# A graph network step kernel on one core: filter products as a pair, and an order of stores and waits

## Chip, cores and metric

One Trainium2 chip (trn2), one core of it. The metric is the device time of one execution in microseconds. The engines go by the profile's names: PE is TensorE (PEld its weight loads), DVE is VectorE, ACT is ScalarE, POOL is GpSimd, SP is SyncE, whose queue here issues nearly all plain transfers.

## The reference

Two graph layers over 50000 nodes and 50000 edges, 128 channels, all in float32. `src` is random, `dst` is sorted.

```
h = relu(layernorm(x));  basis = exp(-coef * (edge_weight - centers)^2)      # 50 centres
ef = (softplus(basis @ Wf1 + bf1) - log 2) @ Wf2 + bf2                       # the filter, per edge
agg = segment_sum((h @ W_lin.T)[src] * ef, dst)                              # messages
x1 = x + (softplus(agg @ Wm1 + bm1) - log 2) @ Wm2 + bm2
h = relu(layernorm(x1))
out = x1 + h @ W_self.T + b_self + segment_mean over src of (h @ W_neigh.T + b_neigh)[dst]
```

## The kernel before

The 50000 rows are padded to 50176 and cut into 98 quads of 512 rows (4 tiles of 128). A first stage counts and sorts indices. The second, which the change touches, is a software pipeline of 98 + 18 steps: in step s every engine does one piece of work for each of several quads, of quad s, s - 1 and so on to s - 18. A last stage sums the edge rows by their `src` bins. `over_steps` (line 98) writes the first 20 steps out, then loops of four steps, and again peeled steps at 72 to 75 and at the end; each engine has a `step` function in which the order of its work is written by hand, and semaphores are the only ties between engines. An engine's instructions, and a queue's, run in the order written; a wait holds all that is behind it.

For quad q as edges: POOL gathers rows of `x` by `src` into `xg` (step q, `gather`); DVE makes their statistics (`row_stats`, `row_aggr`); in step q + 1 DVE and ACT make the inverse root, and the filter: TensorE's `filter_up` (line 1105) multiplied the basis by `Wf1` into `u_ps` in step q, ACT makes `clamp`, `exponential` and `logarithm` (`lu`) of it, DVE's `soften` makes `su`, and TensorE's product with `wf2` goes to `filt_ps`, on top of a bias row (`bias_row(filt_ps, 0, 0)`). ACT makes `xn`, TensorE turns it (`turn`, into `turn_ps`), ACT copies it out as `hT` and the filter as `efs` (named `efb` in rows). In step q + 2 TensorE projects `hT` with `wlin` into `proj_ps`; in step q + 3 DVE's `message` multiplies the two into `msgw` and SP stores it (`store_msg`, line 708). A basis tile holds two quads, on partitions 0 to 49 and 64 to 113 (`BASIS_AT`), and ACT makes it in every even step (`make_basis`).

For quad j as nodes, steps j + 7 to j + 13: SP loads four windows of the message table (`load_windows`, line 718, `win`), DVE looks at their `dst` column (`window_dst`, line 873, `rel`), makes one-hots (`one_hots`, `hot`), TensorE sums (`block_sums`, half-height products, line 1118), ACT copies to `aggs`, TensorE makes the nu product (line 1152), `nsu` follows as for the filter, the product with `wm2`, DVE's `residual` (`x1`, `x` in rows), its layer norm (`node_norm`, `comb` in rows), a transpose, `nhT`, and two products with it: with `wneigh` into `neigh_ps`, from which DVE's `hidden_out` (line 906) makes `h1s` that SP stores (`store_h1`, line 703, table `h_table`), and with `wself` into `self_ps`, from which `node_out` makes `y` rows. `y` rows are stored by `store_y` until quad 61 and kept in SBUF from there (step 72 on). `self_ps`, `mlp_ps` and `neigh_ps` are one bank (`node_ps`), so the bias row of `self_ps` may be written only when `hidden_out` has read the neighbour product; its wait is `wait_used(pe, n_hn, s - 10, 1)`, line 1170, ahead of the bias rows of both `filt_ps` and `self_ps`, which are a pair on rows 0 to 2 and 64 to 66.

For quad q as edges again, steps q + 15 to q + 18: SP loads `dst` keys and four windows of h1 rows (`load_keys`, `load_hidden`, `hwin`), DVE makes one-hots (`edge_hots`, `hotT`), TensorE picks rows (`edge_rows`, half-height, line 1130), ACT makes `row_out`, POOL scatters it (line 798).

Eight PSUM banks: 0 `u_ps`, 1 `turn_ps`, 2 `proj_ps`, 3 `filt_ps`, 4 and 5 the window sums and edge rows by halves, 6 `nu_ps`, 7 `node_ps`.

TensorE's order in a step: product with `wself` (s - 11), block sums (s - 8), product with `wm2` (s - 9), edge rows (s - 17), nu (s - 8), `filter_up` (s), product with `wneigh` (s - 11), transpose of `comb` (s - 10), product with `wlin` (s - 2), the two bias rows, product with `wf2` (s - 1), transpose of `xn` (s - 1). SP's: x rows, y store, edge weights in even steps, message windows, keys, hidden windows, message store, h1 store. DVE's begins with `hot`, `hotT`, `h1s`, message and ends with statistics.

## Time and profile before

| | us |
|---|---|
| median of 3 runs | 1825.5 |
| lowest and highest | 1819.09, 1832.73 |
| the profiled execution | 1825.08 |
| its span, first to last instruction | 1822.9 |
| PE busy | 1614.5 (89%) |
| DVE busy | 1478.6 (81%) |
| ACT busy | 1086.3 (60%) |
| POOL busy | 1114.7 (61%) |
| SP: queue of transfers q1 | 255.35 MB, 48.6% of the 16 DMA engines' time |

A busy share is an average over stages with other limits; instructions that only wait or issue a transfer are not counted as busy, so SP has no busy time, and its load has to be read from its own waits and its timeline. A row of the timeline gives the start, the time to the end of the last instruction merged into it, and in brackets the idle time of the engine before it and who ended it. TensorE's weight loads and matmuls overlap; a float32 product has two records for each matmul, and their ends are modelled, so distances between starts are used for what a product takes.

### The profile page before, as it was taken

The page shows a single profiled execution, that of the slowest core. Times are in us where ns is not written, and L with a number is a line of the kernel's source. Part 1 is how long each engine was busy: PE and PEld are TensorE (multiplying, and loading weights), DVE is VectorE, ACT ScalarE, POOL GpSimd, SP SyncE. Part 2 cuts the span into 40 slices and gives each one's busy share as a digit, 9 for nine tenths or more (in the row PEclk, how much of TensorE's full clock was granted, in tenths as well). Part 3 has the DMA queues.
Part 4 walks back from the last instruction along what each step waited for, and adds up shares of the span by engine and source line. Part 5 has one row for each costly group of instructions (what it writes and reads, how often), then busy time and mean ns, then how long its engine had stood idle before and what let it go on. Part 6 is the DMA issues. An engine that isn't in the chain of part 4 may idle for free. (4 is left out here: it accounts for less than half of the span.)

```text
span 1822.9 us, 49666 instructions
## 1 busy us (share of the span) xinstructions
PE 1614.5 (89%) x13156; PEld 1256.6 (69%) x13156; DVE 1478.6 (81%) x4720; ACT 1086.3 (60%) x2615; POOL 1114.7 (61%) x938
## 2 busy tenths in 40 slices
PE   2549769999999999999999999999999648888997
PEld 1223246777777777777777777777787548888997
DVE  8998646888888888888888889888887427777886
ACT  1007677877777777777777777777764103333333
POOL 5990144356666666666666776677743536555676
PEclk9769878999999999999999999999999859999999
DMA  3000035577777777777777776766766539999876
GB/s 83 0 0 1 18 79 147 169 215 210 219 220 224 221 221 214 219 222 222 215 216 215 222 207 201 207 198 200 201 188 176 158 113 267 271 270 273 232 219 174
DMA packets 293579, 333.96 MB, mean 183 GB/s; under 512 B 42220, under 2 KB 233710, under 8 KB 293486
## 3 DMA queue, kind: packets, MB, share of 16 engines
q1 hardware_dynamic: 216654, 255.35, 48.6%
q0 software_dynamic: 25088, 51.83, 10.1%
q10 hardware_dynamic: 51744, 25.70, 4.7%
q8 instruction: 39, 0.64, 0.1%
q14 instruction: 54, 0.44, 0.1%
HBM read 212.96 MB, written 119.75 MB: 183 GB/s over the span
## 5 line engine op out<-in xcount | busy, mean ns | idle before, releaser
L787 POOL DMA_INDIRECT xg<-in_x,srcs x392 | 414.6, 1058 | 372.8 <-issue 317.7
L798 POOL DMA_INDIRECT row_table<-row_out,posq x392 | 385.2, 983 | 168.4 <-issue 113.9
L1273 PE MATMUL psum<-bin_rows,bin_hot 128*128 128x129 f32 x2352 | 293.7, 284 | 49.7 <-DVE bin_hot L1246 49.5
L1273 PEld LDWEIGHTS psum<-bin_rows,bin_hot 128*128 128x128 f32 x2352 | 278.3, 197 | 65.2 <-DVE bin_hot L1246 33.7
L1246 DVE TENSOR_TENSOR bin_hot<-iota,bin_rel 128x1536 f32<-128x1536 f32 x98 | 178.6, 1822 | 5.5 <-DVE bin_rel L1243 0.2
L1130 PE MATMUL psum<-hwin,hotT 64*128 64x128 f32 x2352 | 165.5, 289 | 15.7 <-DMA hwin<-h_table 13.6
L1130 PEld LDWEIGHTS psum<-hwin,hotT 64*128 64x128 f32 x2352 | 147.3, 196 | 29.0 <-issue 12.3
L1030 ACT ACTIVATE xn<-xg,shift,rstd 128x128 f32<-128x128 f32 x392 | 161.0, 493 | 2.4 <-DVE shift L852 2.2
L1118 PE MATMUL psum<-hot,win 64*128 64x128 f32 x2352 | 159.7, 283 | 0.7 <-DVE hot L882 0.7
L1118 PEld LDWEIGHTS psum<-hot,win 64*128 64x128 f32 x2352 | 140.8, 190 | 12.9 <-DVE hot L882 1.0
L1096 PEld LDWEIGHTS psum<-wneigh,nhT 128*128 128x128 f32 x784 | 95.8, 191 | 70.2 <-issue 70.0
L1288 ACT ACTIVATE x<-psum,inverse 128x128 f32<-128x128 f32 x200 | 57.2, 368 | 135.3 <-DVE inverse L1256 135.3
L1109 PE MATMUL psum<-basis,wf 50*128 50x512 f32 x196 | 114.3, 664 | 26.4 <-DVE su L859 20.4
L1036 ACT ACTIVATE nhT<-psum 128x512 f32<-128x512 f32 x98 | 58.5, 597 | 124.8 <-PE psum L1102 115.1
L569 ACT ACTIVATE psum<-psum,cols 128x196 f32<-128x196 f32 x130 | 51.1, 393 | 128.0 <-PE psum L544 128.0
L1096 PE MATMUL psum<-wf,su 128*128 128x128 f32 x784 | 117.9, 295 | 0.0
L1096 PEld LDWEIGHTS psum<-wf,su 128*128 128x128 f32 x784 | 98.8, 198 | 23.3 <-issue 23.3
L1007 ACT ACTIVATE nclamp<-psum,cols 128x512 f32<-128x512 f32 x98 | 67.3, 687 | 79.0 <-PE psum L1152 78.1
L1096 PE MATMUL psum<-wm,nsu 128*128 128x128 f32 x784 | 113.5, 288 | 0.0
L1096 PE MATMUL psum<-wneigh,nhT 128*128 128x128 f32 x784 | 113.0, 287 | 0.0
L1288 ACT ACTIVATE nx<-psum,inverse 128x128 f32<-128x128 f32 x192 | 54.9, 369 | 97.0 <-DVE inverse L1256 97.0
L1152 PE MATMUL psum<-aggs,wm 128*128 128x512 f32 x196 | 109.6, 641 | 2.5 <-ACT aggs L1036 2.5
(174 smaller groups left out, 3702.6 us busy)
## 6 DMA issues: line engine op xcount, KB each, us to landing
bin_rows<-row_table SPq DMA_DIRECT2D x196, 195.0 KB, 3.2
win<-msg_table SPq DMA_DIRECT2D x392, 96.8 KB
hwin<-h_table SPq DMA_DIRECT2D x392, 96.0 KB
msg_table<-msgw SPq DMA_DIRECT2D x98, 258.0 KB
nx<-in_x_nodes SPq DMA_DIRECT2D x98, 256.0 KB
h_table<-h1s SPq DMA_DIRECT2D x98, 256.0 KB
y_table<-ys SPq DMA_DIRECT2D x61, 256.0 KB
out<-xg ACTq DMA_DIRECT2D x50, 256.0 KB, 3.8
```

The source lines that it names most:

```text
L787: nc.gpsimd.indirect_dma_start(out=xg[:, par, t, :], out_offset=None, in_=ins["x"], in_offset=bass.IndirectOffsetOnAxis(ap=srcs[:, par, t: ...
L798: nc.gpsimd.indirect_dma_start(out=row_dram, out_offset=bass.IndirectOffsetOnAxis(ap=posq[:, par, t:t + 1], axis=0), in_=row_out[:, par, t ...
L1007: nc.scalar.activation(c, ups, ACT.Relu, bias=high, scale=-1.0).then_inc(done, 1)
L1030: last = nc.scalar.activation(out[:, t, :], source[:, t, :], ACT.Relu, bias=shift_[:, t:t + 1], scale=rstd_[:, t:t + 1])
L1096: last = nc.tensor.matmul(ps[:, t * P:(t + 1) * P], left[:, t * P:(t + 1) * P], weights_[:], start=(b is None), stop=(b is None or t == QT ...
L1109: nc.tensor.matmul(u_ps[:], wf1[at:at + BASIS, :], basis[at:at + BASIS, slot, :], start=True, stop=True).then_inc(e_u, 1)
L1118: last = nc.tensor.matmul(tile_ps(agg_at, 2 * g + h), win[half_of(h), par, g, w, 0:C], hot[half_of(h), par, g, w, :], start=(w == 0), stop ...
L1130: last = nc.tensor.matmul(tile_ps(rows_at, 2 * g + h), hotT[half_of(h), par, g, w, :], hwin[half_of(h), par, g, w, :], start=(w == 0), sto ...
L1152: nc.tensor.matmul(nu_ps[:], wm1[:], aggs[:], start=True, stop=True).then_inc(n_u, 1)
L1246: nc.vector.tensor_tensor(bin_hot[:, par, :, :, :], iota4[:].rearrange("p (b n) -> p b n", b=2).unsqueeze(2).broadcast_to([P, 2, BTILES, B ...
L1273: last = nc.tensor.matmul(bank[2 * slot + b][:, h * MW:(h + 1) * MW], bin_hot[:, slot % 2, b, w, h * P:(h + 1) * P], bin_rows[:, slot, b, ...
L1288: last = nc.scalar.activation(of_slot(means, slot)[:, t, :], sums_of(slot)[:, t // 2, t % 2, 0:C], ACT.Identity, scale=inverse[:, slot, t ...
```

## The change

Banks: `u` gets a second bank (3) for odd quads, and the projection and the filter product share bank 2. `filter_up` runs in even steps only and issues the products of both quads of the basis tile. TensorE's projection moves from behind the transpose of `comb` to behind the edge rows, with a wait for the evacuated filter, and the filter's bias row also waits for the message of the quad before. SP: `store_h1` moves from the end of a step to behind `load_x`, `store_msg` to ahead of `load_hidden`. DVE: `message` and `hidden_out` come ahead of `edge_hots`, and `window_dst` moves to the end of the step.

```diff
--- before.py
+++ after.py
@@ -663,7 +663,9 @@
                 x_keys, x_win, scattered = sa2("x_keys"), sa2("x_win"), sa2("scattered")
                 x_hot, x_sum, x_src, x_pos, x_rows = sa("x_hot"), sa("x_sum"), sa("x_src"), sa("x_pos"), sa("x_rows")
                 x_ones = sa("x_ones")
-                u_ps, turn_ps, proj_ps, filt_ps, _, _, nu_ps, node_ps = bank
+                u_even, turn_ps, edge_ps, u_odd, _, _, nu_ps, node_ps = bank
+                u_of = (u_even, u_odd)
+                proj_ps = filt_ps = edge_ps
                 self_ps = mlp_ps = neigh_ps = node_ps
                 agg_at, rows_at = 0, 2 * P
 
@@ -757,6 +759,8 @@
                     def step(s, even, odd, pair, slot, late):
                         if there(s - 9):
                             load_x(s - 9, odd)
+                        if there(s - 13):
+                            store_h1(s - 13, odd)
                         if there(s - 12) and not kept(s - 12, late):
                             store_y(s - 12, even)
                         if even == 0 and there(s):
@@ -765,12 +769,10 @@
                             load_windows(s - 7, odd)
                         if there(s - 15):
                             load_keys(s - 15, odd)
+                        if there(s - 3):
+                            store_msg(s - 3, odd)
                         if there(s - 16):
                             load_hidden(s - 16, even)
-                        if there(s - 3):
-                            store_msg(s - 3, odd)
-                        if there(s - 13):
-                            store_h1(s - 13, odd)
                     over_steps(sp, step)
                     for p in range(2):
                         sp.wait_ge(h1_stored[p], 16 * (QUADS // 2))
@@ -927,12 +929,12 @@
                     def step(s, even, odd, pair, slot, late):
                         if there(s - 8):
                             one_hots(s - 8, even)
+                        if there(s - 3):
+                            message(s - 3, odd)
+                        if there(s - 12):
+                            hidden_out(s - 12, even)
                         if there(s - 17):
                             edge_hots(s - 17, odd)
-                        if there(s - 12):
-                            hidden_out(s - 12, even)
-                        if there(s - 3):
-                            message(s - 3, odd)
                         if there(s - 10):
                             square_root(s - 10, nroot, nsquare, n_root, n_square)
                         if there(s - 1):
@@ -957,13 +959,11 @@
                             inverse_root(s - 1, factor[:], root[:], rstd[:], e_factor, e_norm, e_rstd)
                         if there(s - 10):
                             inverse_root(s - 10, nfactor, nroot, nrstd, n_factor, None, n_rstd)
-                        if there(s - 7):
-                            window_dst(s - 7, odd)
                         if there(s - 10):
                             node_norm(s - 10, even)
                         if there(s - 1):
                             mean_shift(s - 1, emv[:, odd, :, :], rstd[:], shift[:], e_rstd, e_shift)
-                            soften(s - 1, u_ps[:], bf1_low, ln_out[:], su[:], e_softln, e_filter, e_soft)
+                            soften(s - 1, u_of[odd][:], bf1_low, ln_out[:], su[:], e_softln, e_filter, e_soft)
                         if there(s - 9):
                             residual(s - 9, odd)
                         if there(s):
@@ -981,6 +981,8 @@
 
                             wait_used(dve, n_ln, s - 9, 1)
                             row_aggr(s - 9, nstats, nmv, n_stats, n_aggr)
+                        if there(s - 7):
+                            window_dst(s - 7, odd)
                     nc.vector.memset(row_out[:], 1.0).then_inc(x_ones, 1)
                     dve.wait_ge(x_ones, 1)
                     take_src(0, 0)
@@ -1072,7 +1074,7 @@
                         if there(s - 9):
                             logarithm(s - 9, neu[:], nlu[:], n_exp, n_soft, n_softln)
                         if there(s - 1):
-                            clamp(s - 1, u_ps[:], bf1_top, clampu[:], e_u, e_clamp)
+                            clamp(s - 1, u_of[odd][:], bf1_top, clampu[:], e_u, e_clamp)
                             exponential(s - 1, clampu[:], eu[:], e_clamp, e_exp)
                         if even == 0 and there(s):
                             make_basis(pair, slot)
@@ -1102,11 +1104,12 @@
                             last = nc.tensor.transpose(turn_ps[:, t * P:(t + 1) * P], source[:, t, :], ident[:])
                         last.then_inc(done, 1)
 
-                    def filter_up(q, par, pair, slot):
+                    def filter_up(q, pair, slot):
+
                         pe.wait_ge(basis_ready, pair + 1)
                         wait_used(pe, e_soft, q, 1)
-                        at = BASIS_AT[par]
-                        nc.tensor.matmul(u_ps[:], wf1[at:at + BASIS, :], basis[at:at + BASIS, slot, :], start=True, stop=True).then_inc(e_u, 1)
+                        for par, at in enumerate(BASIS_AT):
+                            nc.tensor.matmul(u_of[par][:], wf1[at:at + BASIS, :], basis[at:at + BASIS, slot, :], start=True, stop=True).then_inc(e_u, 1)
 
                     def block_sums(j, par):
                         pe.wait_ge(n_hot, j + 1)
@@ -1146,12 +1149,15 @@
                             if there(s - 8):
                                 pe.wait_ge(n_aggT, s - 8 + 1)
                             edge_rows(s - 17, odd)
+                        if there(s - 2):
+                            pe.wait_ge(e_filter_sb, s - 2 + 1)
+                            product(s - 2, proj_ps, hT, wlin, None, e_hT, e_msg, e_proj)
                         if there(s - 8):
                             pe.wait_ge(n_aggT, s - 8 + 1)
                             wait_used(pe, n_soft, s - 8, 1)
                             nc.tensor.matmul(nu_ps[:], wm1[:], aggs[:], start=True, stop=True).then_inc(n_u, 1)
-                        if there(s):
-                            filter_up(s, even, pair, slot)
+                        if even == 0 and there(s):
+                            filter_up(s, pair, slot)
                         if there(s - 11):
                             pe.wait_ge(n_y, s - 11 + 1)
                             if there(s - 9):
@@ -1164,14 +1170,13 @@
                                 pe.wait_ge(e_hT, s - 2 + 1)
                             wait_used(pe, n_hT, s - 10, 1)
                             turn(nxn, n_turned)
-                        if there(s - 2):
-                            product(s - 2, proj_ps, hT, wlin, None, e_hT, e_msg, e_proj)
                         if there(s - 10):
                             wait_used(pe, n_hn, s - 10, 1)
                             if at_first(s - 10, 1):
                                 pe.wait_ge(n_x1, s - 9 + 1)
                         if there(s - 1):
                             wait_used(pe, e_filter_sb, s - 1, 1)
+                            wait_used(pe, e_msg, s - 1, 1)
                             bias_row(filt_ps, 0, 0)
                         if there(s - 10):
                             bias_row(self_ps, 2, HALF)
```

## Rows read from the trace of the kernel before

**Rows 1.** The head of the page, and its row of the scatters

```profile
span 1822.9 us, 49666 instructions
...
L798 POOL DMA_INDIRECT row_table<-row_out,posq x392 | 385.2, 983 | 168.4 <-issue 113.9
```

**Rows 2.** The windows: us; busy time of each engine; PEclk; DMA share; GB/s

```profile
381.00:1045.00 664.00, 653.78 (x5684) 508.39 (x5682) 579.09 (x2327) 508.13 (x1105) 451.01 (x441) 1.00 0.75 219
1045.00:1349.00 304.00, 303.68 (x2670) 237.71 (x2669) 270.13 (x1081) 236.50 (x516) 210.63 (x204) 1.00 0.70 200
```

**Rows 3.** Waits of SP's queue, 381:1045: us in total, times, longest

```profile
SPq L81 <- DVE hotT L917: 0.6, 1, 0.6
```

**Rows 4.** Waits of SP's queue, 1045:1349

```profile
SPq L81 <- DVE hotT L917: 12.5, 13, 2.4
```

**Rows 5.** Line 1152 in 381:1043 and in 1042:1349: ns min/median/max, first to last start

```profile
L1152 PE MATMUL psum<-aggs,wm x112: 592/645/697, 381.3 to 1042.5; 128*128 128x512 f32 x112
...
L1152 PE MATMUL psum<-aggs,wm x54: 592/645/697, 1041.9 to 1348.7; 128*128 128x512 f32 x54
```

**Rows 6.** Timeline of PE, part of one step: start us, us, engine, line, out<-in

```profile
1016.89 1.61 PE L1130 MATMUL psum<-hwin,hotT 64*128 64x128 f32 x24
1018.43 1.12 PE L1152 MATMUL psum<-aggs,wm 128*128 128x512 f32 x2
1019.48 1.12 PE L1109 MATMUL psum<-basis,wf 50*128 50x512 f32 x2
1020.54 1.16 PE L1096 MATMUL psum<-wneigh,nhT 128*128 128x128 f32 x8
1021.53 0.60 PE L1102 MATMUL psum<-ident,comb 128*128 128x128 f32 x4
1021.97 1.06 PE L1096 MATMUL psum<-wlin,hT 128*128 128x128 f32 x8
1022.96 0.39 PE L1086 MATMUL psum<-bias,ones 3*128 3x512 bf16 x2
```

**Rows 7.** Timeline of DVE in the same step

```profile
1015.01 0.22 DVE L876 TENSOR_SCALAR rel<-win,qhalf 128x6 f32<-128x6 f32 x1
...
1019.76 0.93 DVE L882 TENSOR_TENSOR hot<-iota,rel 128x768 f32<-128x768 f32 x1
...
1021.73 0.69 DVE L910 TENSOR_TENSOR h1s<-psum,bneigh 128x512 f32<-128x512 f32 x1 [0.17 <-PE psum L1096]
```

**Rows 8.** Waits, 381:1045: us in total, times, longest

```profile
DVE rel L876 <- DMA win<-msg_table: 20.0, 22, 1.9
...
DVE h1s L910 <- DMA h_table<-h1s: 8.9, 16, 1.5
```

**Rows 9.** Timeline after the last filter product: two steps, transpose to bias row

```profile
1369.68 0.60 PE L1102 MATMUL psum<-ident,comb 128*128 128x128 f32 x4
...
1370.96 0.38 PE L1086 MATMUL psum<-bias,ones 3*128 3x512 bf16 x1 [0.68 <-DVE h1s L910]
...
1417.57 0.60 PE L1102 MATMUL psum<-ident,comb 128*128 128x128 f32 x4
1417.77 0.69 DVE L910 TENSOR_TENSOR h1s<-psum,bneigh 128x512 f32<-128x512 f32 x1 [0.47 <-PE psum L1096]
...
1418.52 0.38 PE L1086 MATMUL psum<-bias,ones 3*128 3x512 bf16 x1 [0.35 <-DVE h1s L910]
```

**Rows 10.** Timeline of SP's queue in the last steps

```profile
1440.95 2.47 SPq L754 DMA_DIRECT2D hwin<-h_table  x4
1443.53 0.52 SPq L706 DMA_DIRECT2D h_table<-h1s  x1
...
1447.46 2.91 SPq L754 DMA_DIRECT2D hwin<-h_table  x4
```

**Rows 11.** Timeline while the steps fill

```profile
262.91 0.39 PE L1086 MATMUL psum<-bias,ones 3*128 3x512 bf16 x1
...
265.00 0.66 DVE L870 TENSOR_TENSOR msgw<-psum,efb 128x512 f32<-128x512 f32 x1
```

## The prediction

> **What bounds the kernel now.** I read the table of windows first, then the waits engine by engine, then SP's own queue, and last the timeline of single steps. The profiled span is 1822.9 us [rows 1], and the change touches only the big stage of 116 steps.
>
> TensorE looks like the bound: in 381 to 1045 us it is busy 653.78 of 664 us, in 1045 to 1349 us 303.68 of 304 [rows 2]. But the nu product (line 1152, two records a step) gives the length of a step. Its 112 records are 56 steps, so 55 distances from 381.3 us to 1042.0 us (a step's first record starts 0.5 us before its second, the last one listed): 12.01 us a step. The 54 records of the second stretch are 26 distances from 1041.9 to 1348.2 us: 11.78 us a step [rows 5]. The work on TensorE is the same in both, so in the first stretch something else adds 0.23 us a step, some 12 us.
>
> SP's queue is what differs. In the first stretch it waits 0.6 us in 664 [rows 3]: it issues without a pause, and is the limit. In the second, where `y` rows stay in SBUF and their store is gone, it waits 12.5 us in 304 [rows 4], so its own work is (304 - 12.5) / 25.8 = 11.3 us a step, and TensorE leads with 11.78. SP's lateness comes through where VectorE waits for its transfers: 22 times for window rows (20.0 us), 16 times for the store of the h1 buffer (8.9 us) [rows 8]. I call the stretches SP-led and TensorE-led.
>
> **The change part by part.**
>
> *The pair.* The filter product takes 1020.54 - 1019.48 = 1.06 us a step [rows 6]. After the change an even step issues two on the row halves 0 to 49 and 64 to 113, into two banks, and an odd step none. Two such halves run beside each other here: the 24 half-height records of the edge sums take 1018.43 - 1016.89 = 1.54 us, while 8 full-height ones take 1021.53 - 1020.54 = 0.99 us, so 24 in a row would take 2.97; and a pair of bias rows is busy 0.39 us where a single one is 0.38 [rows 6, 9]. I take 1.06 us for the pair, and so 0.53 us less a step. The bounds are 0 gained (the halves queue) and 0.53.
>
> The Trainium skill bears on this (TensorE: Matmul & The Clock Gate, Part 3: matmuls on distinct row groups run concurrently), and the trace agrees. Against single-row-group products stands another page, TensorEngine Tiling, Key Properties: changing the tiling mode drains the engine. By that rule the change would save two drains more in an odd step; but the filter product follows the full-height one before it and precedes the one behind it at 1.05 and 1.06 us, and no drain is seen, so nothing is added.
>
> *The projection moves ahead of nu.* Its 0.99 us (1022.96 - 1021.97) [rows 6] is neither added nor removed, but it was the cover of a wait. The bias rows overwrite the bank of the neighbour product, so they wait for VectorE to have made `h1s` from it. Between the two stood the transpose and the projection: 1.43 us. After the change only the transpose, 1021.97 - 1021.53 = 0.44 us. What the wait needs is seen in the last steps, where there is no projection either: transpose at 1417.57, `h1s` at 1417.77 as soon as the product is there, bias at 1418.52 [rows 9]. That is 0.95 us with VectorE waiting ready, so 0.95 - 0.44 = 0.51 us of new idle time of TensorE in every step. Queued behind it are the filter product, the transpose of `xn` and the whole next step. This is the crux: 0.53 us saved, 0.51 paid. Bounds of the price: 0, if something I don't see covers it, and 0.9, if VectorE is late by another 0.4 us.
>
> Is VectorE late? In this order it does the window look, `hot`, the message and then `h1s`. It is free at 19.76, where `hot` starts now; with 0.22 for the look, 0.93 for `hot` and 0.69 for the message (as long as `h1s`) [rows 7], it could start `h1s` at 21.6 at the latest. The neighbour product ends in an even step 0.99 us later than now (`h1s` at 22.72) and in an odd one 1.06 earlier than that (21.66), so TensorE's result comes last in both, by 0.1 us in the odd ones. An even step is thus 11.78 + 0.51 = 12.29, an odd one 12.29 - 1.06 = 11.23, the mean 11.76.
>
> *The new wait of the filter's bias row on the message.* The projection now shares the filter's bank. The message comes before `h1s` on VectorE and both are waited for at the same place, so this costs nothing beyond the 0.51. Its cover is gone only while the steps fill: there the bias row ran at 262.91 and the message of that step at 265.00, held up by gathered rows [rows 11]. Against it stands the odd filter product being ready a step early. I take 0, bounds 4 us gained and 5 lost.
>
> *SP's order.* No issue is added or taken away, so SP's 12.01 us a step in the SP-led stretch stay. What changes is how far the engines can run ahead of it. The h1 store goes out some 10 us earlier in a step, which ends the 8.9 us of waits for it [rows 8]; it depends on `h1s` of the step before, which is long done. The message store moves ahead of the four hidden loads, and the message is done by then. Moved past: the hidden loads start one issue later, with a step of slack. The next to be late is the window load, and the look at it moves from 1015.01 to just before `hot` at 1019.76 [rows 7]: 4.75 us more slack. TensorE at 11.76 gains 0.25 us a step on SP's 12.01, 13.8 us in 55 steps, so it uses up the 4.75 us once, after 19 steps, and then keeps SP's pace. In the TensorE-led stretch SP (11.3) catches up. So the SP-led stretch gives 4.7 us; bounds 0 (other waits appear at once) and 12 (it is freed altogether).
>
> *The TensorE-led stretch.* 26 steps at -0.02: 0.5 us.
>
> *The last steps.* From 1349 to 1416 us there is no filter work; transpose to bias takes 1370.96 - 1369.68 = 1.28 us, since `hotT` stands before `h1s` on VectorE [rows 9]. After the change `h1s` comes first: 0.95, so 0.33 us in each of 7 steps, 2.3 us. Behind that, steps are a chain on SP: hidden load at 1440.95, h1 store at 1443.53, and the next hidden load waits for it to land until 1447.46, 6.51 us [rows 10]. With the store ahead of the hidden load that landing is hidden, and the scatters are the limit, 4 * (0.98 + 0.30) = 5.1 us [rows 1]. 1.4 us in three steps, I take 3.5 with what surrounds them; bounds 0 and 6.
>
> *Sum.* 4.7 + 0.5 + 2.3 + 3.5 = 11.0 us less. The profiled execution took 1825.08 us against the median of 1825.5, so 1825.08 - 11.0 = 1814.1: 1814.
>
> **The rivals.**
>
> *The stalls go altogether* (15 in 100). SP's pace was set by its neighbours rather than by itself, and the engines hold 11.76 everywhere: 0.25 * 55 = 13.8 in place of 4.7, so 1805. For it: steps of 11.75 occur between longer ones in that stretch. Against: SP's 0.6 us of waits [rows 3].
>
> *The h1s wait is covered* (12 in 100). TensorE then runs at 11.25 a step, but SP needs 11.3: in 26 steps 0.48 * 26 = 12.5 us less in place of 0.5, the SP-led stretch as before: 1802. Against it stands the 0.95 us of rows 9. Both together, with 0.53 us in 81 steps (43 us) and 6 of the last ones, would give 1776 (5 in 100).
>
> *The wait grows: slower* (9 in 100). On VectorE the look, `hot` and the message now all stand ahead of `h1s`, behind which TensorE waits with only a transpose for cover. If a late window row, or the chain from the residual on, makes VectorE start `h1s` 0.7 us later than TensorE's result allows, a step is 11.76 + 0.7 = 12.46 us: 0.68 * 26 in the second stretch and 0.45 * 55 in the first, 42.4 us more, less the 5.8 us of the last steps: 1862. It decides from the point where VectorE is later than TensorE by over 0.25 us a step; there the first stretch stops gaining and the second loses 6 us, and the sum is 1825. Against it: VectorE is busy 579.09 of 664 us [rows 2], 10.5 us a step, and has 0.7 us to spare even in an odd step.
>
> *The pair doesn't run beside itself*: then 11.76 becomes 12.29 a step: 0.51 * 26 + 0.28 * 55 - 5.8 = 22.9 us more, 1848 (1 in 100).
>
> **How the numbers follow.** My forecast has 58 in 100, and its own range is 1805 to 1825. A measurement of this kernel tells about 1% from no change, 18 us. Faster by over 1% is below 1807: a tenth of my forecast's weight, half of the first rival, most of the second and the third, 0.29. Slower by over 1% is above 1844: 0.05. Within: 0.66. The range runs from 1794, which takes in the first two rivals, to 1830.
>
> **What would show it.** Right: two filter products (four records) in about 1.06 us in every second step; TensorE idle before the bias pair some 0.5 us a step, released by `h1s`, step lengths alternating near 12.3 and 11.2 after 1045 us; SP still without waits until the `y` stores end, steps of 12.0 there after the first twenty; no waits of VectorE for the h1 store. Wrong: no idle before the bias pair, steps under 11.6 us in the SP-led stretch, or `h1s` starting much later than 0.2 us after the transpose does.

## The result: slower by 0.8%, where 0.6% faster was predicted

The changed kernel takes 1841.41 us, the median of 7 runs (1834.24 to 1846.12). The ratio to the kernel before is 1.0076, 95% interval [1.0055, 1.0097]. The prediction was 1814 with a range from 1794 to 1830: wrong in its sign, and outside its range. By the bound the prediction used (1% either way) the two kernels are not told apart; by the interval the change is slower.

The profiled execution took 1842.63 us, with the spans of the two profiles 17.0 us apart. Its page's head, and its windows (us; busy time of PE, PEld, DVE, ACT, POOL; PEclk; DMA share; GB/s) over the fill up to the kernel before's first node step, the stretch in which SP led and the one in which TensorE led:

```profile
span 1839.9 us, 49693 instructions
...
221.00:286.00 65.00, 37.18 (x147) 25.46 (x148) 28.41 (x134) 41.98 (x90) 33.05 (x35) 0.63 0.33 85
...
381.00:1062.00 681.00, 631.34 (x5768) 509.27 (x5768) 591.61 (x2359) 515.72 (x1119) 457.50 (x444) 0.99 0.75 215
1062.00:1346.00 284.00, 269.24 (x2474) 216.94 (x2473) 253.03 (x1011) 220.18 (x480) 198.79 (x192) 1.00 0.73 201
```

Beside [rows 2], TensorE is no longer busy all the time: 50 of 681 us are idle now, where it was 10 of 664. It has less work, as meant, and waits longer.

The measure for all that follows is the nu product (line 1158 now, 1152 before), two records a step. Here are its first nine steps and the 57 from the ninth on, first and last start, in the kernel after:

```profile
L1158 PE MATMUL psum<-aggs,wm x18: 592/594/596, 293.4 to 380.8; 128*128 128x512 f32 x18
...
L1158 PE MATMUL psum<-aggs,wm x114: 592/594/596, 380.4 to 1062.3; 128*128 128x512 f32 x114
```

and the first nine of the kernel before:

```profile
L1152 PE MATMUL psum<-aggs,wm x18: 592/594/697, 285.6 to 369.0; 128*128 128x512 f32 x18
```

A step's second record starts 0.4 to 0.5 us after its first, so 114 records span 56 distances: 681.9 - 0.4 = 681.5, 12.17 us a step. Read this way for every kernel of this study (positions are starts of a step's second record):

| kernel | 1st nu | 9th nu | 9th to 65th, a step | 65th to 89th, a step | 89th to 98th |
|---|---|---|---|---|---|
| before | 286.1 | 369.0 | 673.5, 12.03 | 282.7, 11.78 | 91.0 |
| after | 293.8 | 380.8 | 681.5, 12.17 | 284.0, 11.83 | 88.9 |

The difference builds up as +7.7 us at the first nu, +11.8 at the ninth, +19.8 at the 65th, +21.1 at the 89th, +19.0 at the 98th. From there to the last scatter it is 62.6 us instead of 61.1. From the last scatter to the end, which the change doesn't touch, it is 342.1 us instead of 345.6; over all kernels here it lies between 336.2 and 345.6, so that much of a single span says nothing.

**The steps after the fill.** TensorE's timeline after, a step with the pair and one without (the next follows with its pair):

```profile
1156.47 1.02 PE L1158 MATMUL psum<-aggs,wm 128*128 128x512 f32 x2
1157.42 1.13 PE L1112 MATMUL psum<-basis,wf 50*128 50x512 f32 x4
1158.48 1.16 PE L1098 MATMUL psum<-wneigh,nhT 128*128 128x128 f32 x8
1159.48 0.60 PE L1104 MATMUL psum<-ident,comb 128*128 128x128 f32 x4
1160.53 0.39 PE L1088 MATMUL psum<-bias,ones 3*128 3x512 bf16 x2 [0.45 <-DVE h1s L912]
...
1168.74 1.02 PE L1158 MATMUL psum<-aggs,wm 128*128 128x512 f32 x2
1169.60 1.05 PE L1098 MATMUL psum<-wneigh,nhT 128*128 128x128 f32 x8
1170.49 0.60 PE L1104 MATMUL psum<-ident,comb 128*128 128x128 f32 x4
1171.60 0.39 PE L1088 MATMUL psum<-bias,ones 3*128 3x512 bf16 x2 [0.51 <-DVE h1s L912]
...
1177.62 1.61 PE L1133 MATMUL psum<-hwin,hotT 64*128 64x128 f32 x24 [0.27 <-issue]
```

and VectorE's, for the same two steps:

```profile
1157.93 0.68 DVE L872 TENSOR_TENSOR msgw<-psum,efb 128x512 f32<-128x512 f32 x1
1159.78 0.69 DVE L912 TENSOR_TENSOR h1s<-psum,bneigh 128x512 f32<-128x512 f32 x1 [1.16 <-PE psum L1098]
...
1170.26 0.69 DVE L872 TENSOR_TENSOR msgw<-psum,efb 128x512 f32<-128x512 f32 x1
1170.87 0.68 DVE L912 TENSOR_TENSOR h1s<-psum,bneigh 128x512 f32<-128x512 f32 x1
```

Four records, two products, take 1158.48 - 1157.42 = 1.06 us: the pair runs beside itself. Behind the transpose TensorE waits 0.45 and 0.51 us for `h1s`. Step lengths alternate, 12.27 (12.17 in the long stretch) and 11.42 or 11.50. Note the second `h1s`: it has no idle time ahead of it. VectorE, not TensorE's product, comes last in the steps without a pair. These are of two kinds by turns: one waits 0.51 us for `h1s` and then 0.27 us ahead of the edge rows (11.42), the other waits 0.83 us for `h1s` (11.50).

The distances between starts show more. The product behind the transpose started 0.44 us after it [rows 6]. Now the bias row stands there, and starts 1.05 us after it in a step with the pair (1159.48 to 1160.53) and 1.11 or 1.43 us in the others. Over the 24 steps from the 65th nu to the 89th the mean is 1.17, so the uncovered wait costs 0.73 us a step. On the other side, the products next to the filter product got shorter where it is gone: nu takes 1169.60 - 1168.74 = 0.86 us instead of 1.06 (0.95 in front of the pair), and the neighbour product 0.89 instead of 0.99. So a step without the pair has 1.35 us less work, one with it 0.10 less, 0.73 us in the mean. Gain and loss are of one size, and the steps are 11.83 us instead of 11.78.

**The long stretch.** The waits from 381 to 1062 us (us in total, times, longest), and below them SP's own:

```profile
PE psum L1088 <- DVE h1s L912: 27.3, 54, 0.9
PE psum L1133 <- ACT aggs L1038: 21.3, 22, 2.1
DVE su L861 <- ACT lu L1018: 16.1, 21, 1.9
ACT junk L1000 <- DMA ew<-in_ew_pairs: 14.8, 21, 1.7
...
SPq L81 <- DVE hotT L919: 7.4, 4, 4.3
```

The two waits of [rows 8] are gone, for window rows and for the h1 store. In their place stands a chain that wasn't there before: the edge weights come late (14.8 us), so ScalarE's basis is late, then `lu`, then the evacuated sums, and TensorE waits for these 22 times. The steps with the pair are 12.17 us here with hardly an exception; the others vary from 11.1 to 14.7, with 12.16 in the mean.

**The fill.** TensorE's timeline while the steps fill:

```profile
239.18 2.08 PE L1098 MATMUL psum<-wlin,hT 128*128 128x128 f32 x8 [3.43 <-ACT efb L1038]
...
267.22 0.58 PE L1088 MATMUL psum<-bias,ones 3*128 3x512 bf16 x1 [2.86 <-DVE msgw L872]
```

The filter's bias row waits for the message, and the projection for the evacuated filter: the two sides of one bank that two products share now. These waits may also cost clock. Of the same 65 us TensorE was busy 41.52 in the kernel before,

```profile
221.00:286.00 65.00, 41.52 (x180) 26.94 (x181) 29.02 (x136) 43.01 (x92) 34.54 (x36) 0.73 0.34 90
```

at a mean granted clock of 0.73, and 37.18 after, at 0.63. Between the two levels, 1.2 and 2.4 GHz, a larger part is at the lower one. There the eight records of a product take 2.08 us, as at 239.18, behind 3.43 us of idle time, and not 1.16. TensorE was idle for 27.8 of the 65 us, where it was 23.5. How much of the 7.7 us is waits and how much clock can't be told from this.

### The profile page after: what moved, and what is told of

Same layout as the page of the kernel before. It is cut to its first block and busy times, and to the rows that moved or that the text cites. A ratio compares the mean times of both kernels' runs of the same rounds, so it can differ in the third digit from the quotient of the medians.

```text
span 1839.9 us, 49693 instructions
## 1 busy us (share of the span) xinstructions
PE 1562.4 (85%) x13156; PEld 1245.0 (68%) x13156; DVE 1488.4 (81%) x4720; ACT 1087.8 (59%) x2615; POOL 1120.2 (61%) x938
## 5 line engine op out<-in xcount | busy, mean ns | idle before, releaser
L800 POOL DMA_INDIRECT row_table<-row_out,posq x392 | 389.6, 994 | 164.0 <-issue 114.8
L1098 PEld LDWEIGHTS psum<-wneigh,nhT 128*128 128x128 f32 x784 | 99.8, 193 | 57.8 <-issue 57.6
L1088 PE MATMUL psum<-bias,ones 3*128 3x512 bf16 x294 | 80.4, 389 | 68.3 <-DVE h1s L912 51.4
L1098 PE MATMUL psum<-wlin,hT 128*128 128x128 f32 x784 | 118.4, 296 | 13.4 <-ACT efb L1038 13.4
L1098 PEld LDWEIGHTS psum<-wlin,hT 128*128 128x128 f32 x784 | 99.3, 199 | 27.4 <-ACT efb L1038 17.1
L912 DVE TENSOR_TENSOR h1s<-psum,bneigh 128x512 f32<-128x512 f32 x98 | 67.3, 687 | 60.9 <-PE psum L1098 59.7
```

The lines of the kernel that those rows point to most:

```text
L800: nc.gpsimd.indirect_dma_start(out=row_dram, out_offset=bass.IndirectOffsetOnAxis(ap=posq[:, par, t:t + 1], axis=0), in_=row_out[:, par, t ...
L912: nc.vector.tensor_tensor(h1s[:, par, :, :], neigh_ps[:].rearrange("p (t c) -> p t c", t=QT), bneigh[:].unsqueeze(1).broadcast_to([P, QT, ...
L1088: nc.tensor.matmul(ps[:], ones3[at:at + 3, :], bias3[at:at + 3, b, :], start=True, stop=False)
L1098: last = nc.tensor.matmul(ps[:, t * P:(t + 1) * P], left[:, t * P:(t + 1) * P], weights_[:], start=(b is None), stop=(b is None or t == QT ...
```

## The experiments

All ratios are to the kernel before, run beside each kernel on the same chip. The kernel before had medians from 1824 to 1830 us beside them, so kernels that were not run together are compared by their ratios. The positions are those of one profiled execution, whose time can differ from the median: by 6.5 us in e16, which was profiled in its fastest run, and by 5.8 us in e11, profiled in one of its slower ones. A summary first, from the nu product as above:

| kernel | ratio [interval] | 1st nu | 9th nu | us a step, 9th to 65th | 65th to 89th |
|---|---|---|---|---|---|
| e0_both_orders | 1.0574 [1.0546, 1.0602] | 288.0 | 375.6 | 13.20 | 13.20 |
| e1_sp_order | 0.9968 [0.9950, 0.9986] | 286.9 | 371.9 | 12.10 | 11.79 |
| e3_pair_only | 1.0356 [1.0330, 1.0382] | 292.8 | 378.6 | 12.59 | 12.56 |
| e4_all_but_sp | 1.0139 [1.0109, 1.0168] | 292.7 | 381.2 | 12.06 | 11.95 |
| e5_self_bias_late | 1.0066 [1.0047, 1.0084] | 291.0 | 379.7 | 12.18 | 11.84 |
| e6_hidden_first | 1.0021 [0.9995, 1.0047] | 292.6 | 381.5 | 12.00 | 11.82 |
| e7_fill_bank | 1.0061 [1.0037, 1.0084] | 288.0 | 380.1 | 12.19 | 11.83 |
| e8_ew_on_act | 1.0153 [1.0121, 1.0186] | 293.4 | 382.4 | 12.29 | 12.27 |
| e10_fill_rows | 1.0029 [1.0005, 1.0053] | 286.5 | 377.5 | 12.00 | 11.82 |
| e11_before_ew_on_act | 0.9889 [0.9859, 0.9920] | 287.7 | 368.5 | 11.80 | 11.78 |
| e12_h1_store_first | 0.9928 [0.9897, 0.9959] | 286.2 | 370.1 | 11.97 | 11.78 |
| e13_both | 0.9855 [0.9811, 0.9899] | 283.2 | 367.3 | 11.89 | 11.78 |
| e14_pair_ew_on_act | 0.9956 [0.9935, 0.9976] | 287.0 | 377.1 | 11.80 | 11.83 |
| e15_neigh_early | 0.9981 [0.9960, 1.0002] | 285.5 | 374.2 | 11.88 | 11.85 |
| e16_neigh_early_alone | 1.0100 [1.0069, 1.0132] | 292.8 | 382.0 | 12.08 | 11.85 |
| e17_neigh_before_pair | 0.9858 [0.9827, 0.9889] | 286.7 | 378.5 | 11.66 | 11.62 |

### The parts of the change by themselves

**e0_both_orders**: the kernel before with the new orders on SP and VectorE, without the pair and without the projection's move.

```
 VectorE: one_hots, message, hidden_out, edge_hots, ..., row_aggr(s - 9), window_dst
 SP:      load_x, store_h1, store_y, load_ew, load_windows, load_keys, store_msg, load_hidden
```

> Kernel before with SP's and VectorE's new orders, without the pair: TensorE's order and banks are those of before. My theory (the loss comes from the pair's banks and the projection that moved: a wait for the message while the steps fill, and 0.5 us of idle time before the bias rows in each step) says the fill is as before and the h1s wait is covered by the projection again: the time is that of before or up to 6 us less (1819 to 1826), with SP still issuing without a pause up to 1045 us. The rival (the new order of SP is what costs, since SP is the limit there and its register load behind the message store takes 0.58 us instead of 0.28) says 55 steps of 12.1 instead of 12.0 us, so 5 to 10 us more than before (1831 to 1836).

Measured: 1930.69 us. Its waits from 480 to 1040 us:

```profile
DVE msgw L870 <- PE psum L1096: 84.3, 43, 2.0
...
PE psum L1086 <- DVE h1s L910: 56.8, 41, 1.4
```

Every step is 13.20 us. With the projection in its old place, directly ahead of the bias rows, the message waits 2 us for it, `h1s` stands behind the message, and TensorE waits 1.4 us for `h1s`. SP's order alone is e1 below, so VectorE's order is what costs here. The message ahead of `h1s` on VectorE is affordable only with the projection moved.

**e1_sp_order**: the kernel before with the new order on SP alone.

> Kernel before with SP's new order alone. My theory: the waits of VectorE for the h1 store (8.9 us) vanish, but the look at the window rows stays in mid step, so SP's lateness comes through there as before: within 5 us of before. The rival that SP's order costs by itself: 5 to 10 us more than before, 12.1 us a step in the stretch to 1045 us.

Measured: 1822.72 us, a little faster (0.3%). The long stretch is longer (12.10 a step instead of 12.03), with more waits for window rows than in [rows 8]:

```profile
DVE rel L876 <- DMA win<-msg_table: 36.8, 32, 1.9
```

The gain is at the end: from the 89th nu to the 98th 88.6 us instead of 91.0, from there to the last scatter 57.4 instead of 61.1.

**e3_pair_only**: the changed kernel with the old orders on SP and VectorE.

> The pair alone (TensorE's order, banks and waits of after), with SP's and VectorE's orders of before. My theory: the fill costs what it does in after (some 12 us up to 381 us), and the wait for h1s grows beyond after's, since hotT and h1s now stand ahead of the message on VectorE and TensorE waits for the message: 0.7 us more in a step, so slower than after, 1850 or more. The rival (SP's order is the cost): about before's time plus 0 to 5 us, 1826 to 1831.

Measured: 1891.37 us. Steps with the pair are 12.86 us, the others by turns 11.76 and up to 13.8. TensorE's wait is now for the message (480 to 1040 us):

```profile
PE psum L1088 <- DVE msgw L872: 54.0, 45, 1.6
```

The shared bank makes TensorE wait for the message as well, and with `hotT` and `h1s` ahead of it on VectorE that is 1.2 us a step. Against e4, which differs from it by VectorE's order alone, it is 40 us slower: the pair needs VectorE's new order, and e0 shows that the order needs the moved projection.

**e4_all_but_sp**: the changed kernel with SP's old order.

> After with SP's order of before. My theory: the fill and the TensorE-led stretch are as in after (12 us more than before, steps of 12.27 and 11.42). In the SP-led stretch the wait of ScalarE for the edge weights is what holds in after; with the h1 store back behind the hidden loads the waits for it come back too, so the time is that of after within 6 us (1836 to 1847). The rival (SP's order is the cost): 5 to 10 us less than after, 1831 to 1836.

Measured: 1851.43 us. VectorE waits for the h1 store (480 to 1040 us), more than in [rows 8]:

```profile
DVE h1s L912 <- DMA h_table<-h1s: 20.8, 14, 2.7
```

The long stretch is shorter than in the change (12.06), the rest longer: 95.1 us from the 89th nu to the 98th instead of 88.9, and 68.6 us from the 98th nu to the last scatter instead of 62.6. So SP's new order is worth some 11 us to this kernel in all, although it costs in the long stretch. What it costs there is the next question.

### What lengthened the long stretch

**e6_hidden_first**: the changed kernel, two calls on SP exchanged.

```
                             load_keys(s - 15, odd)
+                        if there(s - 16):
+                            load_hidden(s - 16, even)
                         if there(s - 3):
                             store_msg(s - 3, odd)
-                        if there(s - 16):
-                            load_hidden(s - 16, even)
```

> The changed kernel with one edit on SP: the hidden load stands in front of the message's store again instead of directly behind it, all else as changed. Theory (SP sets the length of the SP-led stretch, and its reading of the hidden load's four start rows takes 0.3 us longer directly behind the full 128-row store): SP's step falls from 12.12 to about 11.9, the stretch of 56 steps gets 8 to 12 us shorter, total about 1832. Rival (the stretch got longer because the edge weights' load stands later and the basis is late on ScalarE): nothing but the order behind it changes, the stretch stays at 12.17 a step and the total at 1841. The tail may lose 1 to 2 us, since the last hidden loads no longer wait only for their own store.

Measured: 1830.48 us. The stretch falls from 681.5 to 672.1 us:

```profile
L1158 PE MATMUL psum<-aggs,wm x114: 592/594/595, 381.0 to 1053.5; 128*128 128x512 f32 x114
```

That is 9.4 us for one exchange, with the same DMAs. The rows of SP's queue show where SP's time went. In the change (start us, us):

```profile
876.09 0.35 SPq L713 DMA_DIRECT2D msg_table<-msgw  x1
877.59 2.45 SPq L756 DMA_DIRECT2D hwin<-h_table  x4
```

and with the hidden load ahead of the store:

```profile
867.56 1.12 SPq L741 DMA_DIRECT2D dst_keys<-in_dst_halves  x2
869.57 2.42 SPq L756 DMA_DIRECT2D hwin<-h_table  x4
```

From the end of the issue before it to the first hidden load, SP takes 877.59 - 876.44 = 1.15 us behind the message's store, and 869.57 - 868.68 = 0.89 behind the keys. Over 480 to 1040 us the median of this gap is 1.22 us in the change (46 cases) and 1.21 in e1 (46), against 0.89 in the kernel before, in e6 and in e12 (47 each). In this gap SP reads the four start rows of the load into registers, and that read is what got longer. In the change, and in e6 (ns min/median/max):

```profile
L245 SPq TENSOR_LOAD <-first_row x46: 299/574/754, 486.7 to 1034.9; - x46
...
L245 SPq TENSOR_LOAD <-first_row x47: 133/299/514, 485.3 to 1036.4; - x47
```

Its median is 299 ns in the kernel before too. Why it takes longer behind a store of 128 rows than behind the small broadcast of keys isn't settled; that it follows the order is. Per step of the same 560 us SP's issues take 8.22 us in the kernel before and 8.06 in the change, its gaps 3.81 and 4.11. With the exchange undone, e6's 12.00 is the kernel before's pace again.

The rival had the late edge weights as the cause. They were a symptom: with SP back on its pace, waits of the edge rows for ScalarE fall from 19.3 us (21 times) to 12.0 (12 times) in 480 to 1040 us, with the edge weights' place unchanged. Not all of it is gone: ScalarE still waits 7.4 us for them there.

**e8_ew_on_act**: the changed kernel; the edge weights' DMAs leave SP and are issued by ScalarE behind the basis.

```
                         nc.scalar.activation(basis[:, slot, :], distance, ACT.Exp, scale=-coef).then_inc(basis_ready, 1)
+                        if not isinstance(j, int) or j + 1 < QUADS // 2:
+                            act.wait_ge(squared, j + 1)
+                            for half in range(2):
+                                act.dma_start(ew[64 * half:64 * half + 64, 0, :], ins["ew_pairs"][2 * (j + 1) + half, :]...)
```

> The changed kernel with one edit: the two DMAs a pair that load the edge weights are issued by ScalarE right behind the basis that read the last ones, two steps ahead of need, instead of by SP. Theory (SP sets the stretch from 381 to 1045 us): SP has one DMA a step less, about 0.5 us, and no load waits for the h1 and y stores any more; TensorE takes over, the step falls from 12.17 to about 11.83 there, 19 us over 56 steps, and the total is about 1822. Rival (TensorE's own waits for h1s and for the projection set it already, SP only follows): ScalarE loses the time of the issues, the step stays at 12.1 to 12.2, the total is 1838 to 1845.

Measured: 1855.34 us, slower, and nearer to the rival, which had 1838 to 1845. SP is no longer the limit (it waits 30.6 us for `hotT` from 480 to 1040 us), but ScalarE pays in the middle of a chain that others wait for:

```profile
1016.11 1.13 ACTq L1008 DMA_DIRECT2D ew<-in_ew_pairs  x2
1017.34 0.72 ACT L1022 ACTIVATE lu<-eu,cols 128x512 f32<-128x512 f32 x1 [0.77 <-issue]
```

Steps without a pair are now 12.3 to 12.5 us nearly everywhere, between the 65th and the 89th nu too, where they were 11.46 before this edit. The run says nothing about what SP's relief is worth, so the place was changed for the next ones.

**e11_before_ew_on_act**: the kernel *before*; the same two DMAs, issued by ScalarE in odd steps ahead of the evacuation of the node transposes, where it waits for TensorE anyway.

```
+                        if even == 1 and there(s + 1):
+                            next_ew(pair)
                         if there(s - 11):
                             evacuate(s - 11, nhT[:], turn_ps[:], n_turned, n_neigh, n_hT, ACT.Relu)
```

> The kernel before with one edit: the edge weights' two DMAs a pair are issued by ScalarE in its odd steps, ahead of the evacuation of the node transposes, where ScalarE waits 1.4 us a step for TensorE (62.5 us, 44 times), instead of by SP; with the issues directly behind the basis they had lengthened the changed kernel's odd steps to 12.38. Theory (SP's own work sets the stretch from 381 to 1045 us in the kernel before): SP has one DMA a step less, some 0.4 to 0.5 us; the step falls from 12.03 to TensorE's 11.8, 11 to 14 us in 56 steps, total about 1814. Rival (SP follows, and the stretch is set by the loads' latencies and the engines): the stretch stays within 3 us of 673.5, total 1824 to 1830.

Measured: 1807.58 us, 1.1% faster than before, from one DMA a step fewer on SP (two in every second step). The stretch and SP's waits in it (381 to 1029 us):

```profile
L1159 PE MATMUL psum<-aggs,wm x114: 592/594/697, 368.0 to 1029.5; 128*128 128x512 f32 x114
...
SPq L81 <- DVE hotT L917: 17.2, 36, 1.2
```

661.0 us, 11.80 a step, where it was 673.5: the SP-led stretch is gone, and the steps are TensorE's 11.78 from end to end. The reading of [rows 3] as a limit is shown. The Trainium skill (Trainium Kernel Development and Optimization, Key Constraints) says that issuing DMAs from several engines only saves the sequencer's issue time; here that saving is worth 12.5 us in this stretch, and e8 shows that it can be spent again on the other queue.

**e12_h1_store_first**: the kernel before; on SP only the h1 store moves to the front, the message's store stays behind the hidden load.

> The kernel before with one edit on SP: the h1 store moves to the front of the step; message's store stays behind the hidden load. It is the order of the whole change's SP part without the hidden load behind the message's store. Theory (the register load directly behind the full store is what costs in the SP-led stretch, and the tail gains from the hidden load that no longer stands behind its own h1 store): the SP-led stretch is 12.03 a step as in the kernel before instead of 12.10, 4 us less than the run with the whole SP order, total 1817 to 1821. Rival: what gained in the tail was the message's store; the stretch is 12.03 but the last steps and the tail are those of before, total 1826.

Measured: 1815.76 us, by the ratios 0.4% better than e1, with intervals that just touch. The stretch is 670.1 us (e1: 677.8; the kernel before: 673.5, so the h1 store in front gives 3.4 us there), and the end keeps most of its gain (88.6 and 59.4 us; e1: 88.6 and 57.4). With e6 this is the second pair of kernels in which the hidden load behind the message's store costs 7.7 to 9.4 us there.

**e13_both**: e12 and e11 together.

> The kernel before with both edits: h1's store first on SP, and the edge weights loaded by ScalarE in its idle place. If SP sets the long stretch and the two gains are independent (11 to 14 us there, 5 to 10 in the last steps and the tail), total 1806 to 1812, faster than both kernels. If SP only follows, 1818 to 1822.

Measured: 1801.81 us, 1.5% faster than before. The two gains (1.1% and 0.7%) add up within the interval. The stretch's mean of 11.89 holds one step of 17.57 us, its first; the others are 11.79.

### What was lost in the fill

**e7_fill_bank**: the changed kernel; for the first 7 quads the filter's second product goes to the bank that nu needs only from step 8 on.

```
-                proj_ps = filt_ps = edge_ps
+                proj_ps = edge_ps
+                def filt_of(q):
+                    return nu_ps if isinstance(q, int) and q <= 6 else edge_ps
...
-                            wait_used(pe, e_msg, s - 1, 1)
-                            bias_row(filt_ps, 0, 0)
+                            if not (isinstance(s, int) and s - 1 <= 6):
+                                wait_used(pe, e_msg, s - 1, 1)
+                            bias_row(filt_of(s - 1), 0, 0)
```

> The changed kernel with one edit in the first 8 steps: there the filter's second product goes to the accumulation bank that the node stage's first product uses only from step 8 on, so neither its bias row waits for the message before it nor the projection for the evacuated filter. The work is the same. Theory (the merging of the projection's and the filter's bank costs the fill 7.7 us up to the first node step and 11.8 us up to the ninth): the first node step comes at 286 to 288 us instead of 293.8, the total is 6 to 10 us less, 1832 to 1835. Rival (the fill is set by the gathers, and was longer because message stands ahead of the other work on VectorE): the first node step stays within 2 us of 293.8, the total within 2 us of 1841.

Measured: 1839.71 us. The first nu comes 5.8 us earlier, as expected, but the ninth only 0.7:

```profile
L1162 PE MATMUL psum<-aggs,wm x18: 592/594/595, 287.6 to 380.1; 128*128 128x512 f32 x18
...
302.32 0.58 PE L1091 MATMUL psum<-bias,ones 3*128 3x512 bf16 x1 [4.68 <-DVE msgw L875]
```

In the first step in which the bank is shared again the bias row waits 4.68 us for the message (2.53 us in the like step of the change, at 305.1). The wait was put off, not removed, and the total stayed within 2 us of the change.

**e10_fill_rows**: e6, and for the first 15 quads the filter's second product goes to the halves of two banks that the edge rows use from step 17 on.

```
+                            if in_rows(s - 1):
+                                for h in range(2):
+                                    nc.tensor.matmul(bank[4 + h][:, rows_at:rows_at + 2 * P], ones3[0:3, :], bias3[0:3, 0, 0:2 * P], start=True, stop=False)
+                            else:
+                                wait_used(pe, e_msg, s - 1, 1)
+                                bias_row(filt_ps, 0, 0)
```

> Against the run with the hidden load in front of the message's store (1830.5 us) one edit: for the first 15 quads, so in the whole fill, the filter's second product goes to the halves of the two banks that the edge rows use only from step 17 on. Neither its bias row waits for the message then nor the projection for the evacuated filter, in any step up to 16 (the run that had this only up to step 7 got 5.8 us earlier to the first node step and lost 4.7 of them in one wait for the message in step 8). Theory (the merged bank costs the fill its 12 us): first node step at 287, the ninth at 370 to 373 instead of 381.5, total 1820 to 1824. Rival (the fill after the first node step is set by VectorE's order, with h1 and message in front of the look, or by the gathers): the ninth node step at 378 to 381, total 1828 to 1830.

Measured: 1830.26 us against e6's 1830.48, so no gain in the total that can be told. The first nu comes 6.1 us earlier than in e6, the ninth 4.0. What is left in these steps:

```profile
344.74 0.39 PE L1188 MATMUL psum<-bias,ones 3*128 3x256 bf16 x1 [2.93 <-DVE h1s L915]
...
340.12 0.87 DVE L824 BATCH_NORM_STATS2 stats<-xg 128x6 f32<-128x128 f32 x4 [0.65 <-DMA xg<-in_x,srcs]
...
344.00 0.68 DVE L915 TENSOR_TENSOR h1s<-psum,bneigh 128x512 f32<-128x512 f32 x1
```

The wait for the message is gone, and the one for `h1s`, uncovered since the projection moved, stands there: 0.9 to 2.9 us in five steps, 9.3 in all, where the kernel before waited for `h1s` 3.6 us in four of them. So of the 12.5 us by which e6 is late at the ninth nu, the exchange of banks gives back 4.0, and these waits are 5.7 of the 8.5 that are left. Here the rival (ninth nu at 378 to 381, total 1828 to 1830) was nearer than the theory (370 to 373, 1820 to 1824): it named VectorE's order and the gathers, and the rows bear it out. VectorE waits for gathered rows, then does statistics, window look, `hot`, message and `h1s` without a pause, 3.88 us from the first to `h1s` (340.12 to 344.00). In a like step of the kernel before, with the look and the message not ahead of `h1s`, it is 3.01 (316.99 to 320.00).

Four kernels separate the parts of the change at the ninth nu. The pair with TensorE's order alone is 9.6 us late (e3), VectorE's order adds 2.6 (e4 against e3), and SP's new order adds nothing (-0.4, the change against e4).

### What holds a step at 11.8 us

**e5_self_bias_late**: the changed kernel; the self product's bias row, with the wait for `h1s`, stands behind the filter's second product.

```
                             bias_row(filt_ps, 0, 0)
-                        if there(s - 10):
-                            bias_row(self_ps, 2, HALF)
-                        if there(s - 1):
                             product(s - 1, filt_ps, su, wf2, 0, e_soft, e_filter_sb, e_filter, biased=True)
+                        if there(s - 10):
+                            wait_used(pe, n_hn, s - 10, 1)
+                            bias_row(self_ps, 2, HALF)
```

> The changed kernel with one edit on TensorE: the bias row of the self product, and its wait for the h1 rows, stand behind the filter's second product instead of in front of it. Theory (the pair took away the 0.5 us of work that covered the wait for h1s): the wait of 0.45 to 0.51 us a step before the bias pair goes from TensorE, the self bias no longer overlaps the filter's (about 0.31 us more), so a TensorE-led step falls from 11.83 to about 11.65, 4 us in the 24 steps of that stretch; the SP-led stretch stays. Total about 1837, ratio to the kernel before 1.005. Rival (the wait only shows up there, and is set by VectorE's whole step): the wait moves to the filter's second product or the transposes and the step grows by the 0.31 us: 12.1 in the TensorE-led stretch, total 1848 or more.

Measured: 1839.65 us, 11.84 a step in the last stretch: no gain. TensorE doesn't wait for `h1s` any more, but the steps with the pair are 12.22 us of work without a gap, since the second bias row no longer runs beside the first. The others are 11.42 and 11.50 as before, by turns with 0.33 us of idle ahead of the edge rows and 0.32 us ahead of the filter's bias row, for the message. Neither theory had it: what the wait gave back was spent on the bias row and on these two waits.

**e14_pair_ew_on_act**: e10, and the edge weights issued by ScalarE in odd steps ahead of the node clamp, its idle place in this kernel.

> The changed kernel with the hidden load in front of the message's store and the first 15 filter products in free banks (1830.3 us), and one further edit: the edge weights' DMAs are issued by ScalarE in its odd steps ahead of the node clamp, where it waits 1.6 us a step for TensorE. Theory (two limits: SP where odd steps vary, TensorE with VectorE where they are 12.17 to 12.27 and 11.42 to 11.50): the 56 steps fall from 12.00 to 11.83, 9 us, total about 1821, so the change itself is worth nothing against the kernel before with the same relief of SP (1807.6). Rival (the pair gains once SP no longer limits): the 56 steps go below 11.78 and the total below 1812.

Measured: 1814.10 us (ratio 0.9956; e11, the kernel before with the same relief, has 0.9889). The steps are 12.17 to 12.27 and 11.42 to 11.50 through both stretches, 11.80 and 11.83 in the mean, against e11's 11.80 and 11.78. So the pair, in this order of TensorE's products, is worth nothing per step even where SP leaves room, and the fill makes it slower: the ninth nu is 8.6 us later than in e11.

**e16_neigh_early_alone**: the changed kernel; the neighbour product stands directly behind the edge rows, in front of the projection.

> The changed kernel with only that edit: the neighbour product directly behind the edge rows. Theory: the 24 TensorE-led steps fall from 11.83 to 11.6, 5 us; the long stretch stays near SP's 12.1 to 12.17 a step and gains 2 us at most; the fill gains up to 5. Total 1829 to 1835. Rival (the h1 rows' wait was what lengthened the long stretch too, not SP): the 56 steps fall to 11.9 or less, total 1822 or less.

Measured: 1841.38 us (1.0100). The 24 steps are 11.85 us, not 11.6: the theory of the single wait misses. The 56 steps of the long stretch are 12.08, so the rival, 11.9 or less, misses as well.

**e15_neigh_early**: the same edit on e14.

> The run before this one with one edit on TensorE: the neighbour product, whose result VectorE turns into the h1 rows, stands directly behind the edge rows, in front of the projection, instead of behind the filter's pair. Theory (the moved projection and the pair left the h1 rows uncovered): in the steps with the pair the h1 rows no longer wait 1.4 us for the product and the bias row no longer 0.44 us for them; those steps fall from 12.26 to about 11.8. In the other steps VectorE comes to h1 late behind its own work, so 11.42 stays. The mean falls from 11.83 to about 11.6, 18 us over 80 steps, and the fill, whose steps wait 0.9 to 2.9 us at the same place, gets 5 us shorter: total 1797 to 1803. Rival (VectorE sets both kinds of step by its own work): the mean stays within 0.1 of 11.83 and the total within 5 us of the run before.

Measured: 1819.73 us, slower than e14. The steps with the pair fell from 12.17 and 12.26 to 11.71, as the theory said, and the others rose from 11.46 to 12.05, which it didn't. Of such a step:

```profile
1147.80 0.39 PE L1101 MATMUL psum<-bias,ones 3*128 3x512 bf16 x2 [0.81 <-DVE h1s L915]
...
1154.14 1.61 PE L1146 MATMUL psum<-hwin,hotT 64*128 64x128 f32 x24 [0.59 <-ACT aggs L1046]
```

and the waits from 480 to 1040 us:

```profile
ACT nclamp L1017 <- PE psum L1177: 116.2, 47, 2.6
...
DVE nsmall L837 <- ACT nsmall L1036: 49.5, 42, 2.0
```

nu now stands 1 us later in a step. ScalarE's node clamp waits for it (116.2 us; 76.2 in e14), and VectorE for ScalarE's small roots behind the clamp (49.5 us; 14.2 in e14). VectorE comes late to `h1s`, and TensorE waits for that. By these waits it is a loop: nu, ScalarE, VectorE, `h1s`, bias row, TensorE. (The fill gained 2.9 us at the ninth nu.)

**e17_neigh_before_pair**: e14; the neighbour product stands between nu and the pair, so that the pair covers `h1s`, and nu keeps its place.

```
+                        if there(s - 11):
+                            pe.wait_ge(n_y, s - 11 + 1)
+                            if there(s - 9):
+                                pe.wait_ge(n_x1, s - 9 + 1)
+                            product(s - 11, neigh_ps, nhT, wneigh, None, n_hT, n_hn, n_neigh)
                         if even == 0 and there(s):
                             filter_up(s, pair, slot)
```

> The run with the pair, SP relieved and the fill in free banks (1814.1 us, steps 12.17 to 12.27 and 11.42 to 11.50), with one edit on TensorE: the neighbour product stands directly behind the node stage's first product and in front of the filter's pair, so the pair covers the h1 rows in the steps that have it. The node stage's first product stays as early as it was (in the run with the neighbour product ahead of it, ScalarE and VectorE got its result 1 us later, and the other steps rose from 11.46 to 12.05). Theory of single waits (each step is as long as its own uncovered waits make it): pair steps fall to 11.7 to 11.8, the others stay at 11.46, mean 11.6, total 1796 to 1800. Theory of a loop (node product, ScalarE, VectorE, h1 rows, bias row, TensorE, some 11.8 us a step whatever the order): what the pair steps lose comes back in the others, mean 11.75 to 11.85, total 1811 to 1817.

Measured: 1803.17 us, ratio 0.9858, between the two theories, nearer to that of single waits, and as fast as e13. From its timeline, a step without the pair and one with it:

```profile
L1172 PE MATMUL psum<-aggs,wm x114: 592/594/595, 378.1 to 1031.4; 128*128 128x512 f32 x114
...
1137.49 0.60 PE L1117 MATMUL psum<-ident,comb 128*128 128x128 f32 x4
1138.91 0.39 PE L1101 MATMUL psum<-bias,ones 3*128 3x512 bf16 x2 [0.82 <-DVE h1s L915]
...
1149.00 1.13 PE L1125 MATMUL psum<-basis,wf 50*128 50x512 f32 x4
1150.06 0.66 PE L1117 MATMUL psum<-ident,comb 128*128 128x128 f32 x4
1150.65 0.39 PE L1101 MATMUL psum<-bias,ones 3*128 3x512 bf16 x2
```

Where the pair stands behind the neighbour product the bias rows don't wait at all, and the step is 11.71. In the others the wait grew by 0.3 us, from 0.51 and 0.83 us by turns to 0.82 and up to 1.18. They are 11.42 to 11.75 instead of 11.42 to 11.50: of the 0.5 us that the cover saved in two steps, up to a third came back. The mean of 11.66 and 11.62 is the lowest of all. Here the pair earns something, 0.14 and 0.16 us a step against e11, some 12 us in 80 steps; the fill (the ninth nu at 378.5 us instead of 368.5) takes 10 of them.

## Why the prediction was wrong

Step by step, in the order of the prediction:

- **Two stretches, one led by SP, one by TensorE: right.** e11 shows it: SP's relief alone makes the stretch 12.5 us shorter.
- **The pair, 0.53 us a step: right in that the halves run beside each other (1.06 us for two products), too small as a gain.** Between the 65th nu and the 89th it is 0.73 us. The prediction saw nothing at the change between full-height products and the 50-row one, and added nothing. But nu, 1.06 us in front of a filter product, is 0.86 without it, and the neighbour product behind it 0.89 instead of 0.99. What these 0.30 us are, a drain or something else, isn't shown; they go where the filter product goes, so "no drain is seen" was read from too little.
- **The uncovered wait for `h1s`, 0.51 us: right in kind, too small.** By the prediction's own measure, transpose to bias row, it cost 0.51 to 0.61 us in steps with the pair and 0.66 to 1.18 in the others, 0.73 in the mean. The steps with the pair came at 12.27 (forecast 12.29) because two misses of 0.1 us cancel, which is luck. Those without it were forecast at 11.23 and took 11.42 or 11.50. What failed is "TensorE's result comes last in both, by 0.1 us in the odd ones": in every step without the pair VectorE comes last, and in every second one TensorE also waits 0.27 us ahead of the edge rows, behind ScalarE's copy of the sums. A shortened step doesn't shorten their work. The mean was 11.83, not 11.76, and the stretch lost 1.3 us where it was to gain 0.5.
- **"No issue is added or taken away, so SP's 12.01 us a step in the SP-led stretch stay": wrong, and the first of two terms that turned the sign.** The issues were counted, their pitch was taken as fixed. Behind the message's store the hidden load starts 0.3 us later, since its read of four start rows takes 0.57 us and not 0.30. The term was -4.7 us (bounds -12 and 0); measured +8.0, and e6 gives it back (-9.4) with that one exchange. "The next to be late is the window load" failed too: the edge weights' load was, which the same reordering had put behind two stores. The 4.75 us of slack could not be used up when SP itself fell back, and with SP back on its pace (e6) the stretch is only 1.4 us shorter than before, so most of the 4.7 us did not come either.
- **The fill at nothing, bounds -4 and +5: wrong, and the second.** It cost 11.8 us. The prediction saw the message's wait and its late row [rows 11], and set it off against the odd product being ready early. e7 and e10 put 6 us at the first nu, and e10 puts 4 at the ninth, on the shared bank. For the rest, e10 shows the `h1s` wait at 0.9 to 2.9 us in these steps, where VectorE is held by gathered rows and has the look and the message ahead of `h1s`, so 0.95 us of [rows 9] was no bound for it. Those waits add 5.7 us against the kernel before. VectorE's new order has 2.6 of the 11.8 us (e4 against e3); e15, with the neighbour product early, gained 2.9. What is left was not separated.
- **The last steps and the tail, -2.3 and -3.5: near in size for the first, by luck, and wrong for the second.** From the 89th to the 98th nu 2.1 us were gained, though by one long step of before that is gone, not by 0.33 in each of seven. The tail lost 1.5 us. (1.4 us in three steps are 4.2; the forecast took 3.5.) e1 has the 3.7 us that SP's order was to bring there; in the change VectorE makes `hotT` behind the message and `h1s`, and SP waits for it (10.4 us in e1 and 17.0 in the change, from 1340 to 1500 us). e0, which has VectorE's order beside SP's and no pair, lost the gain as well: 61.4 us from the 98th nu to the last scatter, where e1 has 57.4.
- The sum of the terms by the trace: 11.8 + 8.0 + 1.3 - 2.1 + 1.5 = 20.5, less the 3.5 behind the last scatter, which the change doesn't touch: the 17.0 us between the spans.

No rival was right. The slower one had `h1s` late by 0.7 us in every step of both stretches (1862 us). VectorE was late only in the steps without a pair, in the TensorE-led stretch by under 0.6 us in all but two of them, and the larger gain of the pair made up for it; the loss was at two other places.
